# Two attention layers on one core: the hand-written order of pieces on every engine is replaced by another one

## What is computed

```python
# layer 0, 8 heads of 32
xn = ln(x, ln_w, ln_b)
q = softmax(xn @ Wq + bq, over the 32 features of a head)
k = softmax(xn @ Wk + bk + mask, over the 256 rows)
v = (xn @ Wv + bv) * mask
att = einsum('bnhd,bnhl->bhdl', k, v);  y = einsum('bnhd,bhdl->bnhl', q, att)
# layer 1, 16 heads of 16
att = softmax(q k^T + mask, over the keys);  y = att @ v
# both
e = silu(cond) @ W_emb + b_emb;  scale, shift = split(e)
x = x + silu(ln(y) * (1 + scale) + shift) @ W_out + b_out
```

## Time and profile before

| | |
|---|---|
| three runs | 924.19, 924.09, 922.69 us; median 924.09 |
| the profiled execution | 921.15 us, its span 919.4 us |
| busy share of the span | PE 91%, DVE 89%, POOL 81%, ACT 74%, PEld 65% |
| granted TensorE clock, mean | 0.961 |
| instructions | 25193 |

### The profile page before, as it was taken

How to read it: one execution, slowest core, us unless ns; L and a number is a source line. 1 busy time by engine, 2 the same in 40 slices (tenths; PEclk the granted TensorE clock), 3 DMA queues, 4 the chain that set the end, 5 groups by cost and what they waited for, 6 DMA issues and landing times.

```text
span 919.4 us, 25193 instructions
## 1 busy us (share of the span) xinstructions
...
## 2 busy tenths in 40 slices
...
GB/s 189 60 59 13 49 105 140 89 95 93 130 78 95 113 95 105 105 110 98 92 103 99 106 104 102 106 87 108 109 100 110 98 88 90 96 86 110 69 17 35
DMA packets 149306, 85.84 MB, mean 93 GB/s; under 512 B 87478, under 2 KB 141852, under 8 KB 149180
## 3 DMA queue, kind: packets, MB, share of 16 engines
...
...
## 4 chain that ended last, share of the span: by engine, by line
PE 49%; DVE 27%; issue 11%; POOL 7%; ACT 4%; DMA 0%; POOLq 0%; SPq 0%; DVEq 0%; ACTq 0%
PE banks L684 15%; DVE NM L1243 10%; PE banks L831 7%; PE banks L692 7%; PE banks L818 4%; PE banks L807 4%; PE banks L699 3%; DVE st L1144 3%; PE banks L714 2%; PE banks L750 2%; PE banks L761 2%; DVE ST L1212 2%; PE banks L841 2%; POOL Z L1898 1%; POOL ZHL L1905 1%
## 5 line engine op out<-in xcount | busy, mean ns | idle before, releaser
L1243 DVE TENSOR_REDUCE NM<-banks 128x4 f32<-128x1024 f32 x256 | 302.8, 1210 | 14.8 <-PE banks L807 14.2
L1735 ACT ACTIVATE wraw<-banks,uu 128x1024 f32<-128x1024 f32 x154 | 170.1, 1131 | 13.7 <-PE banks L818 12.9
L1735 ACT ACTIVATE PX<-banks,uu 128x1024 f32<-128x1024 f32 x102 | 112.6, 1127 | 9.0 <-PE banks L818 8.3
L1943 POOL TENSOR_TENSOR SH<-ST,SH 128x512 f16<-128x512 f32 x64 | 74.0, 1158 | 49.7 <-ACT SH L1703 49.7
L684 PE MATMUL banks<-wo,SH 128*128 128x256 f16 x768 | 99.4, 282 | 12.4 <-POOL SH L1943 11.7
L1885 POOL TENSOR_TENSOR rs<-ve,nhalf 128x2 f32<-128x2 f32 x128 | 90.7, 709 | 10.6
L1717 ACT ACTIVATE R<-banks,fcs,sqs 128x256 f32<-128x256 f32 x128 | 73.2, 572 | 34.5 <-PE banks L692 32.3
L818 PE MATMUL banks<-SQ,SK 53*128 53x256 f16 x1024 | 93.5, 273 | 6.0 <-DVE NM L1243 3.0
L807 PE MATMUL banks<-SK,SQ 51*128 51x256 f16 x1024 | 91.6, 272 | 7.9 <-DVE NM L1243 4.7
L684 PE MATMUL banks<-wv,ZT 128*128 128x256 f16 x768 | 94.6, 273 | 0.7 <-DVE X L1223 0.6
L684 PEld LDWEIGHTS banks<-wo,SH 128*128 128x128 f16 x768 | 74.4, 101 | 31.0 <-POOL SH L1943 14.8
...
## 6 DMA issues: line engine op xcount, KB each, us to landing
...
```

Source lines behind the costliest of these rows:

```text
L1243: V.tensor_reduce(NMe[:, c, :, 2 * g:2 * g + 2], banks[:, n:n + 2, :].rearrange("p a (h m) -> p a h m", m=T), AX.X, ALU.max, negate=True). ...
L1735: A.activation(px(v % 5), banks[:, n:n + 2, :].rearrange("p a n -> p (a n)"), ACT.Exp, scale=uu[:, 0:1]).then_inc(S["exp"])
L1943: G.tensor_tensor(SH[:, l, 1], ST[:, l], SH[:, l, 0], ALU.subtract).then_inc(S[f"sl{l}"])
```

## The change

No piece is added or removed, and no instruction inside a piece is changed. The same 396 pieces on SP, 1306 on PE, 938 on DVE, 713 on ACT and 516 on POOL stand in another order; leaving in place as many as possible, 161, 363, 263, 167 and 179 of them move. Most move by a few places. The largest moves are in the setup (`wl_o1` 53 places later, `tr_b` 22 earlier), and small pieces such as `rk` (up to 27 later), `am` and `out_` (up to 26 later). `BANK` and `FREED` are new throughout, and `SETUP` lists the new order of the setup.

```diff
@@ BANK
-    "gk0": "27251067011624154630233461074070",
-    "gkt": "25222061020642260002400401631122",
-    "gq0": "55356151420752310004011570231321",
...
+    "gk0": "23623604370120045466610070670120",
+    "gkt": "27512102276527000561010363220604",
+    "gq0": "74502230206431151577004362317201",
...
@@ block.sync
-            x_in(0); x_in(1); x_in(2); ld_m(); ld_c(); ld_w0(); ld_w1(); ld_r(); ld_o1(); ld_o0(); ld_f1(); mbd0()
-            ld_f0(); am(0); am(1); am(2); z0T(0); aug_d(); z0T(1); x_in(3); am(3); x_in(4); z0T(2); am(4); am(5)
-            z0T(3); z0T(4); am(6); am(7); x_in(5); z1T(0); mbd1(); z0T(5); wq(0); x_in(6); wk(0); am(8); rq6(0)
-            rk6(0); z1T(1); x_in(7); z0T(6); wq(1); z1T(2); am(9); rq6(1); wk(1); nT(0); z0T(7); rk6(1); nw(0)
...
+            ld_m(); x_in(0); x_in(1); ld_c(); ld_w0(); ld_w1(); ld_r(); mbd0(); ld_o1(); ld_f0(); ld_o0(); x_in(2)
+            ld_f1(); z0T(0); am(0); am(1); aug_d(); z0T(1); x_in(3); x_in(4); am(2); am(3); z0T(2); am(4); am(5)
+            z0T(3); z0T(4); am(6); x_in(5); z1T(0); z0T(5); wq(0); wk(0); mbd1(); x_in(6); rq6(0); rk6(0); am(7)
+            z1T(1); x_in(7); z0T(6); wq(1); z1T(2); wk(1); rq6(1); am(8); nT(0); z0T(7); rk6(1); nw(0); nr(0)
...
@@ block.tensor
-            pm(); row3(); row1(); row0(); cnd_t(); tr_w0(); bb0(); ar_w0(); row2(); bb1(); col(); fm0(); tr_o0()
-            k0(0); tr_w1(); v0(0); q0(0); tr_f0(); tr_o1(); v0(1); q0(1); ktT(0); ar_f0(); k0(1); ar_o1(); att(0)
-            ar_o0(); qtT(0); k0(2); q0(2); ktT(1); v0(2); y0(0); att(1); ktT(2); qtT(1); ar_w1(); tr_b(); fm1()
-            y0T(0); q0(3); v0(3); qtT(2); att(2); y0(1); k0(3); k0(4); o0(0); v0(4); q0(4); ktT(3); y0(2); ar_b()
...
+            pm(); row1(); row0(); row3(); tr_w0(); row2(); ar_w0(); bb0(); bb1(); cnd_t(); col(); fm0(); tr_w1()
+            q0(0); k0(0); tr_b(); v0(0); tr_o0(); v0(1); tr_f0(); ktT(0); k0(1); att(0); ar_o0(); q0(1); ar_w1()
+            k0(2); qtT(0); ktT(1); ar_f0(); tr_o1(); y0(0); ar_o1(); q0(2); att(1); v0(2); qtT(1); fm1(); y0T(0)
+            q0(3); y0(1); k0(3); k0(4); ktT(2); qtT(2); o0(0); ar_b(); tr_f1(); v0(3); ktT(3); q0(4); att(2)
...
+            ty(30, 0); ty(30, 1); cols(31, 2); pv(31, 0); cols(31, 3); cols(31, 4); pv(31, 1); pv(31, 2)
+            cols(31, 5); cols(31, 6); pv(31, 3); pv(31, 4); cols(31, 7); y1T(30); pv(31, 5); pv(31, 6); pv(31, 7)
+            ty(31, 0); ty(31, 1); o1(29); y1T(31); o1(30); o1(31)
...
@@ block.vector
-            mb0(); s0(0); s0(1); csl_(); mc(); w0m(); fr0(); csT_(); mx_w0(); fr1(); perm(); bc1(); o0m(); w0p()
-            s0(2); p3_(); bm(); wl_v0(); wl_k0(); o1m(); fr2(); wl_q0(); bc0(); w1m(); f0m(); mx_w1(); km(0)
-            q1(0); s0(3); rk(0); qm(0); mx_f0(); v(0); mx_o1(); v(1); mx_o0(); q1(1); km(1); at_(0); qm(1); s0(4)
-            rk(1); rq(0); q1(2); km(2); qm(2); v(2); Y0(0); rk(2); at_(1); s1(0); w1p(); mx_b(); rq(1); o0p()
-            wl_k1(); film0(); wl_o0(); q1(3); f1m(); st0(0); Y0(1); at_(2); qm(3); wl_v1(); km(3); s1(1); x1(0)
-            rk(3); km(4); s2(0); q1(4); wl_q1(); rk(4); fcs_(); st0(1); mb1(); s0(5); qm(4); mx_f1(); o1p(); rq(2)
-            v(3); Y0(2); wl_o1(); s1(2); rq(3); at_(3); x1(1); rq(4); s2(1); Y0(3); v(4); s1(3); bc2(); film1()
...
+            mb0(); s0(0); s0(1); mc(); w0m(); csl_(); mx_w0(); fr0(); fr1(); perm(); w0p(); w1m(); csT_(); p3_()
+            bc0(); wl_q0(); s0(2); bc1(); o1m(); o0m(); wl_k0(); fr2(); wl_v0(); f0m(); bm(); q1(0); km(0)
+            mx_w1(); qm(0); v(0); s0(3); mx_f0(); s0(4); rk(0); mx_o0(); km(1); at_(0); v(1); q1(1); o0p(); rq(0)
+            qm(1); mx_o1(); w1p(); Y0(0); q1(2); rk(1); film0(); mx_b(); qm(2); s1(0); v(2); at_(1); km(2); rq(1)
+            wl_k1(); f1m(); st0(0); q1(3); Y0(1); qm(3); rk(2); wl_o0(); km(3); s1(1); x1(0); mx_f1(); rk(3)
+            km(4); s2(0); fcs_(); at_(2); o1p(); st0(1); s0(5); rk(4); rq(2); wl_q1(); v(3); q1(4); rq(3); Y0(2)
+            qm(4); s1(2); at_(3); x1(1); mb1(); wl_v1(); s2(1); Y0(3); bc2(); s1(3); km(5); film1(); st0(2); rk(5)
...
+            o_(27); s3(28); max_(31, 0); max_(31, 1); max_(31, 2); max_(31, 3); max_(31, 4); max_(31, 5)
+            max_(31, 6); max_(31, 7); np_(31); st1(28); Y1_(29, 0); Y1_(29, 1); s3(29); o_(28); st1(29)
+            Y1_(30, 0); Y1_(30, 1); s3(30); Y1_(31, 0); Y1_(31, 1); s3(31); st1(30); st1(31); o_(29); o_(30)
+            o_(31)
...
@@ block.scalar
-            th(); wh_v0(); wh_q0(); wh_k0(); ke(0); kt(0); qe(0); qt(0); ke(1); qe(1); kt(1); ke(2); kt(2); qt(1)
-            wh_k1(); qe(2); wh_q1(); wh_o0(); wh_v1(); th0(0); qt(2); sh0(0); ke(3); ke(4); kt(3); th0(1); kt(4)
-            sh0(1); wh_o1(); qe(3); qa(0); qt(3); qe(4); ka(0); qt(4); th0(2); sh0(2); ke(5); kt(5); qe(5); qt(5)
...
-            yt(30, 1); yt(30, 2); th1(29); yt(30, 3); sh1(29); exp(31, 0); exp(31, 1); exp(31, 2); exp(31, 3)
-            exp(31, 4); yt(31, 0); exp(31, 5); exp(31, 6); exp(31, 7); yt(31, 1); yt(31, 2); th1(30); yt(31, 3)
-            sh1(30); th1(31); sh1(31)
...
+            th(); wh_k0(); wh_v0(); wh_q0(); ke(0); kt(0); ke(1); qe(0); qt(0); wh_o0(); kt(1); qe(1); wh_k1()
+            qt(1); qe(2); th0(0); ke(2); sh0(0); kt(2); ke(3); wh_q1(); wh_v1(); qt(2); kt(3); ke(4); th0(1)
+            sh0(1); qe(3); qa(0); qt(3); ka(0); qe(4); kt(4); th0(2); qt(4); ke(5); sh0(2); kt(5); qe(5); wh_o1()
...
+            exp(30, 4); exp(30, 5); exp(30, 6); exp(30, 7); yt(30, 1); yt(30, 2); th1(29); yt(30, 3); exp(31, 0)
+            exp(31, 1); exp(31, 2); exp(31, 3); exp(31, 4); exp(31, 5); exp(31, 6); exp(31, 7); yt(31, 0)
+            yt(31, 1); yt(31, 2); yt(31, 3); sh1(29); th1(30); sh1(30); th1(31); sh1(31)
 
...
@@ block.gpsimd
-            nmz(); cst(); fill(); r0(0); r0(1); z0(0); z0(1); r0(2); xb0(0); z0(2); xb0(1); v1z(); r0(3); qs(0)
-            z0(3); qs(1); r0(4); z0(4); qs(2); r1(0); yn0(0); sl0(0); qs(3); r1(1); xb0(2); yn0(1); xb1(0); r2(0)
-            z1(0); sl0(1); r0(5); z0(5); qs(4); r1(2); spq(0); yn0(2); xb0(3); spk(0); r2(1); r1(3); z1(1); sl0(2)
...
+            nmz(); cst(); fill(); r0(0); r0(1); z0(0); z0(1); xb0(0); r0(2); xb0(1); z0(2); r0(3); qs(0); z0(3)
+            qs(1); r0(4); z0(4); r1(0); yn0(0); qs(2); v1z(); sl0(0); qs(3); r1(1); xb0(2); yn0(1); r2(0); z1(0)
+            xb1(0); sl0(1); r0(5); z0(5); qs(4); r1(2); spq(0); yn0(2); xb0(3); spk(0); r2(1); xb1(1); r1(3)
...
+            yn1(27); spq(31); vm(30); sl1(27); xb1(30); r3(28); yn1(28); sl1(28); r3(29); yn1(29); vm(31); r3(30)
+            yn1(30); sl1(29); r3(31); yn1(31); sl1(30); xb1(31); sl1(31)
```

More of the change, by code:

```diff
@@ L87 @@
-    "ga_b": "7",
-    "gfm0": "0",
-    "gfm1": "7",
+    "ga_f1": "1",
+    "gt_b": "1",
+    "ga_b": "5",
+    "gfm0": "1",
+    "gfm1": "5",
 }
@@ L94 @@
     "gk0": (
[L95 to L96 removed]
+        "p3 v:1 bm film0 qt:2 at:4 ka:2 x1:4 max:14 exp:9 max:32 vt:6 th0:10 exp:45 qt:14 ka:11 exp:68 o:8 ka:14 "
+        "vt:14 max:112 yt:53 Y1:28 qa:19 exp:132 exp:141 max:162 max:167 max:176 x1:26 qa:26 ka:27 "),
     "gkt": (
[L98 removed]
@@ L253 @@
     "PE": (
-        "pm row3 row1 row0 cnd tr_w0 bb0 ar_w0 row2 bb1 col fm0 tr_o0 tr_w1 tr_f0 tr_o1 ar_f0 ar_o1 ar_o0 "
-        "ar_w1 tr_b fm1 ar_b tr_f1 bb2 ar_f1 ").split(),
+        "pm row1 row0 row3 tr_w0 row2 ar_w0 bb0 bb1 cnd col fm0 tr_w1 tr_b tr_o0 tr_f0 ar_o0 ar_w1 ar_f0 "
+        "tr_o1 ar_o1 fm1 ar_b tr_f1 ar_f1 bb2 ").split(),
     "DVE": (
-        "mb0 csl mc w0m fr0 csT mx_w0 fr1 perm bc1 o0m w0p p3 bm wl_v0 wl_k0 o1m fr2 wl_q0 bc0 w1m f0m mx_w1 "
-        "mx_f0 mx_o1 mx_o0 w1p mx_b o0p wl_k1 film0 wl_o0 f1m wl_v1 wl_q1 fcs mb1 mx_f1 o1p wl_o1 bc2 film1 ").split(),
+        "mb0 mc w0m csl mx_w0 fr0 fr1 perm w0p w1m csT p3 bc0 wl_q0 bc1 o1m o0m wl_k0 fr2 wl_v0 f0m bm mx_w1 "
+        "mx_f0 mx_o0 o0p mx_o1 w1p film0 mx_b wl_k1 f1m wl_o0 mx_f1 fcs o1p wl_q1 mb1 wl_v1 bc2 film1 wl_o1 ").split(),
     "ACT": (
-        "th wh_v0 wh_q0 wh_k0 wh_k1 wh_q1 wh_o0 wh_v1 wh_o1 ").split(),
+        "th wh_k0 wh_v0 wh_q0 wh_o0 wh_k1 wh_q1 wh_v1 wh_o1 ").split(),
     "POOL": (
@@ new lines, in _ @@
+            cols(11, 5); cols(11, 6); pv(11, 2); pv(11, 3); pv(11, 4); pv(11, 5); rows(13, 1); rows(13, 2)
+            cols(11, 7); y0(17); ktT(19); ty(11, 0); y1T(10); att(18); pv(11, 6); pv(11, 7); rows(13, 3)
+            cols(12, 0); cols(12, 1); v1p(14); ty(11, 1); cols(12, 2); cols(12, 3); q1p(15); rows(13, 4)
+            rows(13, 5); pv(12, 0); pv(12, 1); rows(13, 6); k1p(15); o1(10); cols(12, 4); rows(13, 7); o0(16)
+            y0T(17); qtT(19); k0(20); v0(20); q0(20); cols(12, 5); rows(14, 0); rows(14, 1); pv(12, 2); pv(12, 3)
@@ new lines, in _ @@
+            v1p(18); ty(15, 1); qtT(23); pv(16, 0); pv(16, 1); rows(17, 5); cols(16, 2); q1p(19); rows(17, 6)
+            cols(16, 3); o0(20); o1(14); cols(16, 4); rows(17, 7); k1p(19); y0T(21); k0(24); v0(24); q0(24)
+            cols(16, 5); rows(18, 0); rows(18, 1); pv(16, 2); pv(16, 3); pv(16, 4); pv(16, 5); cols(16, 6)
```

(2 more changed lines are left out.)

803 lines of the change are left out of this document (390 added, 413 removed), and 210 rows, old and new, of the table FREED.

## The result

The changed kernel takes 902.20 us (median of 4 runs, 900.00 to 903.35) against 924.14 us for the kernel before (4 runs). The profiled execution took 900.0 us, the fastest of the four, its span is 898.2, so 21.2 us of span are to be explained.

A forecast was written before the change was run, and what follows sets the result against it. Only PE's idle time (79.4 of 919.4 us) and low-clock work could shrink; DVE, then POOL, bound the opening. 5.3 + 1.05 + 1 + 1.5 = 8.8 us off 921.15, median 2.9 higher: 915.3 us, range 908.5 to 921.5.

The forecast's parts named there:

- Masks first on SP: Opening: second mask lands at 4.94 us, before `fill`'s first long memset; `mb0` ends at 21.4 instead of 26.7, 5.3 us.
- What runs in the freed 5.3 us: Opening, DVE behind `mb0`: statistics and small pieces pass beside the fourth memset; full 5.3 us taken, bounds 0 and 6.0.
- Wait ahead of `bc1`: Opening, DVE: its 1.05 us wait for PE's broadcast goes, as `bc0` and `bc1` now stand later; 1.05 us.
- the order ahead of `s0(5)`: Opening, DVE: 7.0 us of pieces move behind `s0(5)`, which releases POOL's gapless stretch; 1 us taken, bounds 0 and 7.0.
- Middle: The 640 us of the middle: PE's work unchanged and its largest wait short; 0 taken, bounds −4 and +4.
- Closing: Last batches: all `yt(31)` ahead of `th1(30)` on ACT; 1.5 us won, bounds −1 and 2.5.
- The term for `yt(31)`: Closing, ACT: `yt(31)` no longer waits behind `th1(30)`; 1.79 us less, 0.3 more for `yt(31, 0)`, 1.5 us won.
- `o1(29)`: Closing, PE: new ahead of `y1T(31)` and waiting for `sl1(29)`; said to fit closely.
- Rival 3: Opening: all of the moved DVE work pays, POOL's stretch starts 7.0 us earlier; 14.9 us, 909.2 us; chance 0.12.

The follow-up runs named there:

- new_masks_back: Changed kernel with only `ld_m` moved back behind `x_in(1)` on SP: 905.41 us.
- m1_masks_first: Kernel before with one edit, `ld_m` first on SP: 917.72 us.
- new_scattered: Changed kernel with 40 single PE pieces moved one place earlier, between two score pieces, so that shape changes rise from 528 to 608: 914.64 us.
- the splices: Five kernels following one order up to about batch 2, 10 or 27 and the other from there: 926.30, 917.47, 918.77, 916.65 and 919.22 us.
- old_tail_new: Kernel before with the changed order only in its last pieces, from `cols(31, 3)` on PE: 919.25 us.

## Why the prediction was right in direction and wrong in size

Three steps failed. The gain in span exceeded the sum by some 12.3 us: 2.5 in the opening, where the landing of the masks was mis-sized, 3.1 in the middle ("PE's work is the same, so I take 0"), and 6.7 in the closing, by terms that the prediction left out.

- **Masks first on SP.** The mechanism held, and the term was mis-sized. The step that failed is "with the same 3.65 us to landing": with nothing ahead of them the masks landed in 1.70 us, so no CAST met a memset. new_masks_back, with the landing as assumed, shows the rest of the step within 0.2 us.
- **What runs in the freed 5.3 us.** Statistics and TENSOR_REDUCE beside a memset, which no row of before had, pass: 0.75 us for two statistics at 6.79 in the changed kernel and 1.73 us for a TENSOR_REDUCE at 13.90 in m1_masks_first. By the rule that the prediction cites from the page "SBUF — State Buffer" of the Trainium skill (Who interferes with whom) that was due, and the trace agrees. The upper bound of 6.0 was no bound, since it left out that `mb0` could be over before `fill`.
- **Wait ahead of `bc1`, and the order ahead of `s0(5)`.** Not separated. Together with the rest of the setup they give new_masks_back 6.4 us at `q1(0)` (50.5, as predicted) and 6.1 at np(8), where the steps summed to 7.35. That the two steps to `q1(0)` sum to just what was measured may be luck.
- **What the opening's gain is.** It is in the main time won back from the memsets of `fill`: with these on ScalarE the old order is level with the new one. The prediction saw each port-blocked instruction end with a memset, and asked only how the change steers around that.
- **Middle.** "PE's work is the same, so I take 0" failed. The order changes how often PE changes the shape of its matmuls. Between np(8) and np(24) the changes fall from 299 to 255 and PE's busy time by 5.6 us, while its idle time rises by 2.5 (4.7 to 7.2): together the 3.1 us. The price of a change is shown, and new_scattered shows busy time coming back with the changes; 44 x 0.105 = 4.6 us leaves 1.0 of the 5.6 open.
- **Closing.** The term for `yt(31)` was right in size (4.14 to 2.70 us, 1.4) but not the one edit that it was put down to; DVE's `st1(30)` had to move as well, as the change does. The rest of the 8.2 us had no term. Up to np(29) the order gives 2.8 us, also in the splices and in new_masks_back; which moves bring them stays open. From np(29) to np(31) the changed kernel gains 1.3 more because its clock stayed at 1.00, which is luck as far as these runs show: new_masks_back loses 1.9 there. `o1(29)` stood ahead of `pv(31, 0)`, and the prediction looked at it only as a risk:

```profile
892.15 2.72 PE L684 MATMUL banks<-wo,SH 128*128 128x256 f16 x12 [0.70 <-ACT PX L1735]
```

  That is before, at a granted clock of 0.50; at 1.00 such a piece takes 1.48 us, as it does in the changed kernel, which has it behind `ty(31, 1)`. The lead grows by 1.7 us from np(31) to the end of the last `exp` (899.56 against 880.79, 18.8). The tail alone gives 0.8 of them in old_tail_new. And `o1(31)` took 2.74 us before, all at a clock of 0.50, and 2.04 after, where the clock fell to 0.50 only in the middle of it:

```profile
892.75 2.04 PE L686 MATMUL banks<-wo,SH 128*128 128x256 f16 x12 [2.70 <-POOL SH L1945]
```

  So the closing was forecast too small for two reasons of different kind: the order is worth some 4 to 5 us there instead of 1.5, and the clock added 3 to 4.
- **The rivals.** The middle gave nothing back on balance: PE idles 2.9 us more from 160 to 800 us, which its shorter work outweighs. Rival 3, the largest gain considered, was 14.9 us; all four took the busy work as fixed, and so did the range.
